# A routed feed-forward block feeding a GRU: 64-token chunks, resident weights, gate inputs projected straight into the gate banks, and fp32 words streamed as bf16 halves

## The reference

```python
# layer 0, on x of shape (2, 1024, 256)
gate_in = concat([mean over all tokens, mean without the middle third, mean without the first third])
logits  = (gate_in @ gate_w + gate_b) * (1 + scale) + shift      # scale, shift from silu(cond) @ time_w
w_be    = top 2 of softmax(logits), renormalised                 # one weight per sequence and expert
for e in range(4):                                               # mask: e=1 drops the middle third, e=2 the first
    out += w_be[:, e] * mask[e] * (gelu(x @ ew1[e] + eb1[e]) @ ew2[e] + eb2[e])
x = x + out + gelu(x @ sw1 + sb1) @ sw2 + sb2                    # hidden width 1024
# layer 1, one step per token
z  = sigmoid(x_t @ W_z + h @ U_z + cond @ C_z + b_z)
r  = sigmoid(x_t @ W_r + h @ U_r + cond @ C_r + b_r)
hh = tanh(x_t @ W + (r * h) @ U + cond @ C + b)
h  = (1 - z) * h + z * hh
out_t = x_t + h
```

## Time and profile before

| | us |
|---|---|
| median of the runs | 2235.7 |
| profiled execution, first to last instruction | 2236.9 |
| first scan of the recurrence (L730) starts | 124.7 |
| last scan (the 1024th) starts | 2230.9 |
| TensorE busy | 2118.5 |
| VectorE busy | 1200.3 |
| ScalarE busy | 686.9 |
| GpSimd busy | 344.0 |

### The profile page before, as it was taken

How to read it: one execution, slowest core, us unless ns; L and a number is a source line. 1 busy time by engine, 2 the same in 40 slices (tenths; PEclk the granted TensorE clock), 3 DMA queues, 4 the chain that set the end, 5 groups by cost and what they waited for, 6 DMA issues and landing times.

```text
span 2236.9 us, 108229 instructions
## 1 busy us (share of the span) xinstructions
PE 2118.5 (95%) x43019; PEld 1776.9 (79%) x43019; DVE 1200.3 (54%) x10473; ACT 686.9 (31%) x3670; POOL 344.0 (15%) x684
## 2 busy tenths in 40 slices
PE   7999999999999999999999999999999999989998
PEld 6788888888888888888888888888888888765665
DVE  5245555555555555555555555555554555555555
ACT  2333333333333332333333333333333333222222
POOL 3011111111111111111112111111111111110000
PEclk8999999999999999999999999999999999899999
DMA  5411111111111111111111111111111111000000
GB/s 160 133 53 48 44 47 39 44 45 43 49 39 42 49 44 41 44 42 44 47 41 42 46 46 42 41 46 42 44 46 39 42 49 44 12 4 4 4 4 4
DMA packets 143478, 97.21 MB, mean 43 GB/s; under 512 B 13664, under 2 KB 142999, under 8 KB 143004
## 3 DMA queue, kind: packets, MB, share of 16 engines
q1 hardware_dynamic: 141840, 90.49, 14.2%
q10 hardware_dynamic: 1164, 0.07, 0.0%
HBM read 88.41 MB, written 2.10 MB: 40 GB/s over the span
## 4 chain that ended last, share of the span: by engine, by line
PE 88%; DVE 5%; ACT 4%; issue 3%; POOL 0%; POOLq 0%; ACTq 0%; DVEq 0%
PE c_ps L917 21%; PE r_ps L917 20%; PE y_ps L874 16%; PE up_ps L856 13%; PE z_ps L917 12%; DVE h_parts L730 3%; PE up_ps L945 3%; ACT c_ps L507 3%; PE xp_ps L888 2%; DVE p_parts L716 1%; ACT r_ps L507 1%; PE xp_ps L898 1%; PE y_ps L829 0%; DVE hidden L278 0%; PE z_ps L903 0%
## 5 line engine op out<-in xcount | busy, mean ns | idle before, releaser
L917 PE MATMUL r_ps<-h_parts,u_high 128*128 128x20 f16 x8192 | 558.9, 180 | 81.7 <-DVE h_parts L730 49.5
L917 PEld LDWEIGHTS r_ps<-h_parts,u_high 128*128 128x128 f16 x8192 | 424.6, 96 | 261.4 <-DVE h_parts L730 149.3
L917 PE MATMUL z_ps<-h_parts,u_high 128*128 128x20 f16 x8192 | 565.6, 179 | 0.0
L917 PE MATMUL c_ps<-p_parts,u_high 128*128 128x40 f16 x8192 | 526.7, 182 | 14.9 <-DVE p_parts L716 1.9
L856 PE MATMUL up_ps<-feat,up_w 128*128 128x128 f32 (+1 forms) x2380 | 526.6, 314 | 0.0
L917 PEld LDWEIGHTS c_ps<-p_parts,u_high 128*128 128x128 f16 x8192 | 412.8, 96 | 138.4 <-issue 41.0
L874 PE MATMUL y_ps<-hidden,down_w 128*128 128x128 f32 (+1 forms) x2380 | 498.0, 314 | 5.6 <-DVE hidden L278 5.6
L716 DVE SCALAR_TENSOR_TENSOR p_parts<-r_ps,h_hist 128x4 f16<-128x4 f32 x1024 | 166.5, 163 | 528.9 <-ACT r_ps L507 528.3
L917 PE MATMUL z_ps<-h_parts,u_mid 128*128 128x20 f16 x4096 | 438.0, 179 | 0.0
L917 PEld LDWEIGHTS z_ps<-h_parts,u_high 128*128 128x128 f16 x8192 | 424.8, 96 | 0.0
L507 ACT ACTIVATE r_ps<-r_ps 128x4 f32<-128x4 f32 x1024 | 161.8, 158 | 744.5 <-PE r_ps L917 744.4
(11 more groups left out here) (132 smaller groups left out, 2157.9 us busy)
## 6 DMA issues: line engine op xcount, KB each, us to landing
up_w<-in_L_cond_ew SPq DMA_DIRECT2D x256, 128.0 KB, 2.4
down_w<-in_L_cond_ew SPq DMA_DIRECT2D x256, 128.0 KB, 2.1
up_w<-in_L_cond_sw SPq DMA_DIRECT2D x64, 128.0 KB, 2.4
down_w<-in_L_cond_sw SPq DMA_DIRECT2D x64, 128.0 KB, 2.1
x_rows<-in_x SPq DMA_DIRECT2D x8, 256.0 KB, 4.9
out<-out_rows SPq DMA_DIRECT2D x128, 16.0 KB, 1.8
cf<-in_L_cond_C_r SPq DMA_DIRECT2D x1, 256.0 KB, 5.8
cf<-in_L_cond_C_z SPq DMA_DIRECT2D x1, 256.0 KB, 6.0
```

What stands on the lines that cost most here:

```text
L917: return mm(gate_ps[g][:, m * SC + t * B:m * SC + t * B + width], w[:, g, k, m * P:(m + 1) * P], moving, start=False, stop=i == LO and k = ...
```

## The change

The kernel is rewritten around the same arithmetic.

1. The chunk is 64 tokens. All up and down weights stay in SBUF (`up_w`, `down_w`), loaded once by large transfers.
2. The feed-forward of a chunk is 40 tiles (branch, hidden block), four products of 128 columns each, plus two bias products. A table `SIDE` puts one such product in window 0 and two in window 1 of each of the 64 steps, the projections after them.
3. The gate banks hold two regions, one for each of two successive chunks. VectorE writes the gate bias of the next chunk there (`seed`), TensorE adds `x @ W` directly (`project`), and the recurrence adds to it. `xpart`, `split` and `inject` go.
4. VectorE writes h once, as fp32 (`h_cur`), and r*h once, as fp32 (`p_cur`). TensorE streams the upper 16 bits of these words as bf16 (`h_bits`, `p_bits`); the lower part is the difference from them (`h_low`, `p_low`).
5. The tanh results lie in banks of their own. The output addition moves from GpSimd to VectorE, one small instruction per step.
6. The prologue computes chunk 0 alone, 64 tokens, without branch 2, which is masked there.

```diff
-STEPS = 16
+TOKENS = 64
+STEPS = 16
...
+    units = []
+    for i in range(BR * HT + LAG):
+        if i < BR * HT:
+            units += [(UP, i, 0), (UP, i, 1)]
...
+    for t in range(CT):
+        for w in range(2):
+            while units and len(SIDE[t, w]) < 1 + w:
+                SIDE[t, w].append(units.pop(0))
...
-        up_w = sb("up_w", [P, BR, KC, P])
-        down_w = sb("down_w", [P, BR, D])
+        up_w = sb("up_w", [P, BR, KC, H])
+        down_w = sb("down_w", [P, BR, HT, D])
...
+        h_bits = h_cur[:, :, :].bitcast(BF16)
+        p_bits = p_cur[:, :, :].bitcast(BF16)
+        h_now = h_cur[:, 0, 1:2 * ST:2]
+        h_high = h_bits[:, 0, 3:4 * ST:4]
...
-                    dve.wait_ge(act_done, gate0 + 1)
-                    dve.wait_ge(state, s0 - 1)
-                    dve.scalar_tensor_tensor(p(HI), tr, 1.0, prev, ALU.add, ALU.mult).then_inc(part_ready, 1)
-                    dve.scalar_tensor_tensor(sq(product), tr, 1.0, prev, ALU.add, ALU.mult).then_inc(state, 1)
-                    dve.wait_ge(state, s0 + 1)
-                    dve.tensor_tensor(p(LO), sq(product), p(HI), ALU.subtract).then_inc(part_ready, 1)
...
-                    dve.wait_ge(act_done, gate0 + 3)
-                    dve.wait_ge(state, s0 + 3)
...
+                dve.wait_ge(part_ready, parts + H_HIGH)
+                dve.wait_ge(act_done, s * GATES + R + 1)
+                dve.scalar_tensor_tensor(p_cur[:, :, 0:B], sq(tanh_r), 1.0, sq(h_now), ALU.add, ALU.mult
+                                         ).then_inc(part_ready, 1)
+                dve.wait_ge(part_ready, parts + PARTS_STEP + P_HIGH)
+                dve.tensor_tensor(p_low[:, :, 0:B], p_cur[:, :, 0:B], p_bits[:, :, 1:2 * B:2], ALU.subtract
+                                  ).then_inc(part_ready, 1)
...
+                dve.wait_ge(blended, (s + 1) * BLEND_STEP + 2)
+                dve.wait_ge(act_done, s * GATES + C + 1)
+                dve.tensor_tensor_scan(h_cur[:, 0, :], cand, blend[:, :], 0.0, ALU.mult, ALU.add
+                                       ).then_inc(part_ready, 1)
+                dve.wait_ge(part_ready, parts + PARTS_STEP + H_HIGH)
+                dve.tensor_tensor(h_low[:, 0, :], h_now, h_high, ALU.subtract).then_inc(part_ready, 1)
+                dve.tensor_scalar(half_h[:, :], h_now, -0.5, None, ALU.mult).then_inc(blended, 1)
...
+                last = dve.scalar_tensor_tensor(
+                    out_feat[:, body % 2, :, row * B:(row + 1) * B], sq(h_now), h_unscale[:, :],
+                    feat[:, :, s * B:(s + 1) * B], ALU.mult, ALU.add)
...
-            def inject(g, last_of_body):
-                for i in range(3):
-                    last = mm(gate_ps[g][:, 0:KC * SC], ident16[:, :],
-                              xsplit[:, i, g * KC:(g + 1) * KC, :].rearrange("p k n -> p (k n)"),
-                              start=(i == 0), stop=(i == 2), skip_group_check=True)
...
+            def project(c, g, m, k):
+                at = (c % 2) * REGION + m * COLS
+                mm(gate_ps[g][:, at:at + COLS], wx[:, g, k, m * P:(m + 1) * P], feat[:, k, c * COLS:(c + 1) * COLS],
+                   start=False, stop=False, skip_group_check=True)
```

More of the change, by code:

```diff
@@ L68, in moe_gru_kernel @@
     b_in = [b_r, b_z, b_h]
[L72 to L82, removed]
@@ L83, in moe_gru_kernel @@
-    assert not units
[L85 to L93, removed]
@@ new lines, in moe_gru_kernel @@
+    assert not units
+    GELU_STEP = {}
+    for (t, w), some in SIDE.items():
+        for kind, i, k in some:
+            if kind == UP and k == 1:
+                GELU_STEP.setdefault(t + w, []).append(i)
+    RESIDUAL_STEP = DOWN_STEP + 1
+    projections = {w: [(g, m, k) for g in ((C,), (R, Z))[w] for m in range(KC) for k in range(KC)] for w in range(2)}
+    for t in range(RESIDUAL_STEP + 1, CT):
+        for w in range(2):
+            while projections[w] and len(SIDE[t, w]) < 1 + w:
+                SIDE[t, w].append((PROJECT, *projections[w].pop(0)))
@@ L165, in moe_gru_kernel @@
         spread = sb("spread", [B, BR, B])
[L168 to L171, removed]
+        keep_warm = sb("keep_warm", [P, RANK], BF16)
+        h_cur = sb("h_cur", [P, H_FILL // B, 2 * ST])
+        h_low = sb("h_low", [P, H_FILL // B, ST], F16)
+        p_cur = sb("p_cur", [P, KC, FILL])
+        p_low = sb("p_low", [P, KC, FILL], F16)
@@ L338, in _ @@
+            for i in range(2):
+                sp.wait_ge(out_written[i], CH * BODIES // 2 * B * 16)
         @block.gpsimd
@@ L580, in _ @@
+            dve.memset(p_cur[:, :, :], 0.0)
+            dve.memset(p_low[:, :, :], 0.0)
+            dve.memset(h_low[:, :, :], 0.0)
+            dve.memset(h_cur[:, :, :], 0.0).then_inc(part_ready, PARTS_STEP)
             dve.memset(blend[:, :], 0.0)
             link(dve.memset(picked[:, :], 1.0))
-            dve.memset(half_h[:, :], 0.0).then_inc(state, STATE_STEP)
+            dve.memset(half_h[:, :], 0.0).then_inc(blended, BLEND_STEP)
             for e in range(1, E):
-                dve.memset(before[:, e, 0:e], 1.0)
@@ new lines, in _, with residual, side @@
+            dve.memset(cand, 0.0)
+            make_rows(CT, T).then_inc(rows_made, 1)
+            scale_first(24, len(TILES[0]))
+            def residual(c, k):
+                if k == 0:
+                    dve.wait_ge(down_done, TILE0[c + 1])
+                here = feat[:, k, c * COLS:(c + 1) * COLS]
+                dve.tensor_tensor(here, y_ps[:, k * COLS:(k + 1) * COLS], here, ALU.add).then_inc(feat_ready, 1)
+            for k in range(KC):
+                residual(0, k)
+            def side(c, t, window):
+                if c == CH - 1:
+                    return
+                if (t, window) in SEEDS:
+                    seed(c + 1, *SEEDS[t, window])
+                if t == RESIDUAL_STEP:
+                    residual(c + 1, window)
@@ L871, in down @@
[L871 to L892 removed]
+                return last
@@ L910, in _, with recur @@
             LOW_PRODUCTS = [(m, k, u_high) for m in range(KC) for k in range(KC)]
[L912 removed]
+            def recur(s, g, low, product, last_of_sum=False):
                 m, k, w = product
[L915 to L919 removed]
@@ L921, in gap_work @@
[L921 to L943 removed]
+                c, t = divmod(s, CT)
```

922 lines of the change are left out of this document (390 added, 532 removed).

## The result

The changed kernel takes 2187.6 us (median of 4 runs, 2186.0 to 2189.6), the kernel before on the same chip 2236.9: ratio .977, 95% interval .975 to .979. The forecast was 2105, with a range up to 2180. The sign was right, the size was not: 49 us were gained where 132 were forecast.

The account below looks back on a forecast made before the run. The kernel was taken as bound by a ring of latencies of 2.00 us per step, no engine's throughput. Prologue 61 + 1023 steps x 1.99 (2036) + irregular 5 + end 4.5 = 2106, forecast 2105 us; 8 in 10 range 1960 to 2180.

Parts of the forecast that it names:

- The ring: Chain of engine latencies in one recurrence step: from 2.00 us to 1.82, or 1.99 with two late waits at .085 each.
- The streams free: TensorE's upper products reading bf16 words 4 or 8 bytes apart: claimed to cost nothing, still .025 us each.
- The rival at 2526: Upper products of R and C slowed like fp32 streams: step 2.40, total 2526 us; chance .05.
- The free waits (1963): VectorE's separate waits at p_cur and scan nearly free, .015 each: step 1.85, total 1963 us; chance .17.
- the waits at GpSimd's price (2239): VectorE's separate waits at .15 each: step 2.12, total 2239 us, no change; chance .06.
- "So 60 becomes 5.": Irregular steps between scans: 60 us fall to 5, with one gelu stall per chunk of .3, 15 times, left.
- "Short stretches at half clock add 1": Irregular steps: TensorE's time at half clock was put at 1 us in all.
- "the steps around the projections like the others": Sign in the profile after: steps at the projections no longer than ordinary ones, one step in 64 longer by .3.
- "a mean step outside 1.92 to 2.06": Sign that would make the prediction wrong: mean step in us beyond these limits; 1.99 was forecast.
- "The chunk's end stalls as before": Rival: chunk-end steps stall 6 us each, now 15 times, 90 us: total 2195 us; chance .05.
- The prologue at 61: Time before the first scan: from 124.7 to 61 us, with GpSimd's chain hidden by the last tiles.
- The end at 4.5: Time after the last scan: 4.5 us, not 6.0, since L382's detour over GpSimd goes.

Follow-up runs that it names:

- e2_swap: The changed kernel with the two waits of p_cur, blend and scan on VectorE in the other order, ScalarE's tanh first; 2043.1 us, ratio .912.
- e9_packed: As e6_shift, with edit 4 undone: upper halves again written as packed bf16 words of their own by extra VectorE instructions; 2086.2 us, ratio .931.
- e4_before_late: The kernel before, with the two waits of p(HI) and of the scan exchanged so ScalarE's tanh becomes a late separate wait; 2428.6 us, ratio 1.085.
- e7_one_wait: As e1_fill, with the two waits exchanged at the scan alone, not at p_cur and blend; 2039.9 us, ratio .910.
- e5_wx_act: The changed kernel with e1_fill's filler and e2_swap's wait order, and wx scaled on ScalarE instead of GpSimd; 1961.2 us, ratio .875.
- e1_fill: The changed kernel with filler products on TensorE in the windows at each chunk's end that hold no side work; 2117.6 us, ratio .945.
- e6_shift: As e5_wx_act, with each chunk's third tile's up products one window later; 1942.3 us, ratio .867.
- e8_last_bare: As e5_wx_act, but with no filler products in the last chunk; 1970.3 us, ratio .879.

## Why the prediction was wrong, step by step

- **The ring.** Right. Without the waits it was put at 1.82 and e2_swap has 1.833; the waits at .085 each, and they cost .067 to .070. The forecast of 1.99 met 1.973, closer than its parts: the ring was costed a little short and the waits a little dear. The gain of the fourth edit and the price of the waits are both real and nearly equal, 137 and 143 us, which is why so large a change moved the median step by only .027.
- **The streams free.** Right, by the .025 in the changed kernel and by e9_packed. The rival at 2526 is out. The earlier trace rows had shown the spacing of .025 for 4 bytes, and the changed kernel shows it for 8.
- **The free waits (1963), the waits at GpSimd's price (2239).** Both out: .07 lies between them, and e4_before_late and e7_one_wait measure it alone.
- **"So 60 becomes 5."** This step failed. Irregular steps took 95 us. The one stall that was named (.3, 15 times) was there, at .32 (2.29 against 1.97, where the clock was full; .38 with the shorter step of e5_wx_act). "Short stretches at half clock add 1" was the error: the steps that half clock touched hold 86 of the 95, and e1_fill, which only fills the empty windows, gives back 70 us of the time. I had looked for stalls where the windows are overfull and not at windows with nothing in them, though the program puts filler into the last chunk's. The earlier trace rows show TensorE with little idle time, since the kernel before had side work nearly everywhere; its clock was .982. The test "the steps around the projections like the others" failed, and "a mean step outside 1.92 to 2.06" did as well, by .006.
- **"The chunk's end stalls as before", 2195.** The number is near and the reason is not. It put the 90 us to steps overloaded as in the earlier trace rows. e1_fill adds work to that place and the steps get shorter.
- **The prologue at 61.** Off by 7.4 us, in a term of the sum (whose parts, as written, add up to 60.1). GpSimd's chain was put at 36 to 54, "hidden by the last tiles, and if it came 5 later it would be the end". It ran from 40.6 to 61.3. TensorE, idle meanwhile, then did the projections at half clock. Part of the delay is length: its rows took 20.7 instead of 18.5. The rest is its start, 4.2 us later than in the kernel before. That is not the idle time ahead of its first row: it is 7.40 here, but the earlier trace rows has 7.19 at the same place, and the 36 already contains that. What moved is what the chain waits for. The changed kernel writes TensorE's product of the expert weights behind eleven tiles of up products (28.85), so VectorE copies them at 29.39 instead of 23.26, and `umax`, written behind that copy, releases GpSimd's all-reduce at 32.73 instead of 26.82. (2.1 us of GpSimd's own copies, which stood between before, are gone.) This is read from the order of the rows; no run moves that product. The Trainium skill (GPSIMD Engine Reference, section Instruction dispatch) says that a kernel freshly loaded into GpSimd pays about 6 us at its first call, with no row of its own. The gap ahead of the chain's first row (7.40, 7.35 in e5_wx_act, 7.19 before) is of that size; that loading is its cause was not tried. In the kernel before, copies ran between the all-reduce and the gap, so it does not stand directly behind the all-reduce:

```profile
27.18 2.08 POOL L401 COPY gate_scale<-expert_w 128x684 f32<-128x684 f32 x2
```

- **The end at 4.5.** Right, 4.3.

With the two mis-sized terms put right (95 for 5, 68.4 for 61) the sum is 68.4 + 2036 + 95 + 4.5 = 2204, and with the step at 1.973 it is 2186.

The Trainium skill (TensorE: Matmul & The Clock Gate, section HAM oscillation — how this bites in real kernels) tells of kernels whose TensorE falls back to half clock again and again because it waits between bursts. The traces agree that the clock falls in every chunk, 358 us in all. They differ in that TensorE never waits for long here: each step of the empty windows still has 36 small products, and between the first scan and the last no idle time of TensorE is above .57 us.

## What to carry to other kernels

When a change removes side work from an engine that a recurrence leaves half idle, look for windows that become empty: the granted clock of those stretches, and the first full windows behind them, belong in the sum. Here filler in those windows gave back 70 us, and in e6_shift, where a stall behind them went too, no half clock was left. Write the wait that comes last so that it is the one attached to the instruction; a late separate wait in a ring costs VectorE .07 us per pass. When work is put in a new order, look up for every engine what releases its first row: here a product that was written eleven tiles later moved GpSimd's whole chain.

## What the runs showed of the hardware

- A separate wait that comes late costs .067 to .070 us on VectorE, measured in three ways (1.973 to 1.833 for two, 1.974 to 1.904 for one, 2.000 to 2.139 for two in the other kernel). The wait written first was the attached one.
- With nothing on TensorE but the recurrence's small products (36 per step of 1.8 to 2.0 us) the granted clock falls to 1.2 GHz and stays there, from 1838.7 to the end at 1966.1 in e8_last_bare, and most steps take 1.98 in place of 1.83. With filler of 256 and twice 512 bf16 columns per step it stays at 2.4 GHz through the same chunk in e5_wx_act. At chunk ends such filler leaves three falls in e1_fill.
- At half clock the cost is small by itself (.15 a step) and large where side work meets it: 2.65 to 3.10 a step.
- At 2.4 GHz products of 20 or 40 columns are .025 us apart whether their 16-bit words are packed or every second or fourth.
